# A head's softmax sums inverted and applied in their PSUM bank instead of by way of memory

## The reference

```python
q, k, v = split(xn @ qkvw + qkvb)             # 32 heads of 32 columns
scores = einsum('bhqd,bhkd->bhqk', q, k) / sqrt(32)
ctx = einsum('bhqk,bhkd->bhqd', softmax(scores), v)
x + ctx @ ow + ob + ffn(xn)
```

## Time and profile before

| | |
|---|---|
| median of 3 runs | 2800.13 us (2799.02 to 2804.99) |
| the profiled execution | 2805.34 us |
| its span | 2803.3 us |
| mean granted TensorE clock | 0.955 |
| busy, share of the span | PE 94%, DVE 61%, POOL 56%, ACT 44% |

### The profile page before, as it was taken

One profiled execution on the slowest core, in us unless ns is written; L12 is line 12 of the kernel. 1 busy time (PEld: TensorE's weight loads), 2 busy tenths in 40 slices (PEclk: granted clock), 3 DMA queues, 4 the chain that ended last, 5 costly groups with the idle time before them and its releaser, 6 DMA issues. The chain is left out here.

```text
span 2803.3 us, 34972 instructions
## 1 busy us (share of the span) xinstructions
PE 2646.7 (94%) x13032; PEld 1682.0 (60%) x13032; DVE 1701.0 (61%) x2649; ACT 1234.9 (44%) x2299; POOL 1568.3 (56%) x498
## 2 busy tenths in 40 slices
PE   7999999999799999999999999999999999988999
PEld 6888887778455454554555455455545545526887
DVE  8411111111588888888888878888888888823222
ACT  3111111110066565666566666656666666662100
POOL 0111111011078787888788788878878887871221
PEclk9999999999699999999999999999999999998999
DMA  4233333113546667667666766776676667424332
GB/s 143 87 130 124 116 112 113 67 55 103 139 96 140 127 135 150 141 129 152 142 130 138 151 143 129 148 146 130 139 151 141 131 145 150 102 58 161 116 105 94
DMA packets 168168, 351.01 MB, mean 125 GB/s; under 512 B 89632, under 2 KB 114720, under 8 KB 137376
## 3 DMA queue, kind: packets, MB, share of 16 engines
q0 software_dynamic: 22320, 162.54, 28.9%
q1 hardware_dynamic: 145712, 186.70, 24.0%
HBM read 122.44 MB, written 63.69 MB: 66 GB/s over the span
## 5 line engine op out<-in xcount | busy, mean ns | idle before, releaser
L899 DVE TENSOR_REDUCE part_max<-ps_b 128x1 f32<-128x512 f32 x2048 | 1259.8, 678 | 288.2 <-PE ps_b L778 287.9
L736 POOL TENSOR_TENSOR psum_p<-psum_p,probs 128x2048 f32<-128x2048 f32 x254 | 1189.0, 4681 | 76.9 <-ACT probs L885 66.7
L885 ACT ACTIVATE probs<-ps_b 128x512 f32<-128x512 f32 x1924 | 990.0, 616 | 518.4 <-PE ps_b L767 514.0
L778 PE MATMUL ps_b<-kp,qp 96*128 96x512 f32 x2048 | 878.9, 437 | 108.4 <-DVE part_max L899 93.7
L767 PE MATMUL ps_b<-qp,kp 97*128 97x512 f32 x2048 | 866.1, 426 | 5.2 <-ACT probs L885 5.1
L767 PEld LDWEIGHTS ps_b<-qp,kp 97*128 97x128 f32 x2048 | 400.5, 196 | 343.1 <-issue 207.8
L778 PEld LDWEIGHTS ps_b<-kp,qp 96*128 96x128 f32 x2048 | 414.8, 203 | 249.2 <-DVE part_max L899 182.4
L794 PE MATMUL ps_b<-probs,vh 128*32 128x512 f32 x3848 | 484.5, 618 | 0.0
L236 POOL TENSOR_TENSOR wlo<-wraw,whi 128x1024 fp32r<-128x1024 f32 x29 | 69.5, 2399 | 612.9 <-ACT whi L339 612.9
L265 PE MATMUL ps_a<-xhi,whi 128*128 128x512 f32 (+1 forms) x928 | 370.6, 399 | 1.1 <-DVE elo L428 0.9
L265 PE MATMUL ps_a<-xlo,whi 128*128 128x512 f32 (+1 forms) x928 | 367.8, 396 | 0.0
(11 more groups left out here) (78 smaller groups left out, 1226.4 us busy)
## 6 DMA issues: line engine op xcount, KB each, us to landing
psum_q<-probs POOLq DMA_DIRECT2D x155, 1024.0 KB, 7.6
kp<-qk_scr SPq DMA_DIRECT2D x96, 256.0 KB, 4.1
qp<-qk_scr SPq DMA_DIRECT2D x96, 256.0 KB, 6.3
qk_scr<-ehi SPq DMA_DIRECT2D x16, 1024.0 KB, 3.9
qk_scr<-elo SPq DMA_DIRECT2D x16, 1024.0 KB, 6.7
wraw<-wcat SPq DMA_DIRECT2D x29, 512.5 KB, 7.5
craw<-cz_scr SPq DMA_DIRECT2D x16, 768.0 KB, 5.0
stage<-x SPq DMA_DIRECT2D x16, 512.0 KB, 3.9
```

The source lines that it names most:

```text
L736: pool.tensor_tensor(acc[:, :], first[:, :], tile(h, t)[:, :], ALU.add).then_inc(pool_done, 1)
L778: pe.matmul(ps[:, ring_bank(u), :], qp[s][0:PACK, tn * P:(tn + 1) * P], kp[s][0:PACK, b * NQ:(b + 1) * NQ], start=True, stop=True).then_in ...
L885: act.activation(tile(h, t)[:, b * NQ:(b + 1) * NQ], ps[:, n % ST_BANKS, :], ACT.Exp, scale=SCALE).then_inc(exp_done, 1)
L899: dve.tensor_reduce(part_max[hn % 2][:, tn, b:b + 1], ps[:, ring_bank(u), :], AX_X, ALU.max) \
```

## The change

The reciprocals are taken by VectorE in the PSUM bank that holds the sums, in four quarters of 128 columns, in place. Each quarter of the context is then the product of `raw_ctx` (SBUF) and that bank (PSUM). Both happen in the head after the one they belong to, at steps 7 to 10: the reciprocal after the second block's maximum, the multiply after the fourth's. ScalarE's copy of the sums, the spreading, storing and broadcasting DMAs and their semaphores go, and one of three `raw_ctx` buffers. The bank stays out of the ring until the fourth multiply (step 10), so the maxima of steps 7 to 10 have three banks; which bank comes next is now worked out from a list of unused banks. In the last head four reciprocals of 128 columns take the place of one of 512.

```diff
-SUMS_AT, RECIPROCAL_AT, NORMALISE_AT = 6, 9, 1
+SUMS_AT = 6
+DIVIDE_AT = SUMS_AT + 1
+GIVEN_BACK_AT = DIVIDE_AT + QB - 1
...
-        raw_ctx = [sb(f"raw_ctx{s}", [P, NQ]) for s in range(3)]
+        raw_ctx = [sb(f"raw_ctx{s}", [P, NQ]) for s in range(2)]
...
+                if t == GIVEN_BACK_AT and h >= 1:
+                    ring_order.append(("given back", h - 1, 0, 0))
...
+        ring_bank, ring_before, maxima_until = {}, {}, {}
+        unused = [(RING_BANK + n, None) for n in range(RING_BANKS)]
+        maxima = 0
         for u in ring_order:
-            maxima_until.append(maxima_until[-1] + (u[0] == "max"))
-
-        def ring_bank(u):
-            return RING_BANK + ring_place[u] % RING_BANKS
+            if u[0] == "given back":
+                u = ("sum", *u[1:])
+                unused.append((ring_bank[u], u))
+                continue
+            ring_bank[u], ring_before[u] = unused.pop(0)
+            maxima += u[0] == "max"
+            maxima_until[u] = maxima
+            if u[0] != "sum":
+                unused.append((ring_bank[u], u))
...
             elif kind == "sum":
-                eng.wait_ge(sums_taken, h + 1)
+                eng.wait_ge(ctx_ready, QB * (h + 1))
...
-            def invert_sums(h):
-                sp.wait_ge(sums_taken, h + 1)
-                for b in range(QB):
-                    sp.dma_start(sums_q[b * HD:(b + 1) * HD, :], sums_b[b * HD:b * HD + 1, :]) \
-                        .then_inc(sums_spread, 16)
-                sp.wait_ge(recip_done, h + 1)
-                sp.dma_start(recip_scr.rearrange("(p c) -> p c", p=P), recip_q[:, :]).then_inc(recip_stored, 16)
-                sp.wait_ge(recip_stored, 16 * (h + 1))
-                for b in range(QB):
-                    sp.dma_start(recip_b[b * HD:(b + 1) * HD, :],
-                                 recip_scr[b * NQ:(b + 1) * NQ].partition_broadcast(HD)).then_inc(recip_loaded, 16)
...
-                    if h >= 2:
-                        store_ctx(h - 2)
-                    invert_sums(h - 1)
+                    store_ctx(h - 1)
...
-                    if t == SUMS_AT and h >= 1:
-                        take_sums(h - 1)
...
-            def reciprocal(h):
-                dve.wait_ge(sums_spread, 16 * QB * (h + 1))
-                wait(dve, recip_stored, 16 * h)
-                dve.reciprocal(recip_q[:, :], sums_q[:, :]).then_inc(recip_done, 1)
+            def reciprocal(h, part):
+                c = slice(part * P, (part + 1) * P)
+                bank = ps[:, ring_bank[("sum", h, 0, 0)], c]
+                if part == 0:
+                    dve.wait_ge(sum_ready, h + 1)
+                dve.reciprocal(bank, bank).then_inc(recip_done, 1)
...
-                dve.tensor_tensor(out_ctx[h % 2][:, c], raw_ctx[h % 3][:, c], recip_b[:, c], ALU.mult) \
-                    .then_inc(ctx_ready, 1)
+                dve.tensor_tensor(out_ctx[h % 2][:, c], raw_ctx[h % 2][:, c], ps[:, ring_bank[("sum", h, 0, 0)], c],
+                                  ALU.mult).then_inc(ctx_ready, 1)
...
-                        if b == 1 and h >= 2 and 0 <= t - NORMALISE_AT < QB:
-                            normalise(h - 2, t - NORMALISE_AT)
-                    if t == RECIPROCAL_AT and h >= 1:
-                        reciprocal(h - 1)
+                        if h >= 1 and 0 <= t - DIVIDE_AT < QB:
+                            if b == 1:
+                                reciprocal(h - 1, t - DIVIDE_AT)
+                            if b == 3:
+                                normalise(h - 1, t - DIVIDE_AT)
...
-            dve.reciprocal(recip_b[:, :], ps[:, ring_bank(("sum", LAST, 0, 0)), :]).then_inc(recip_done, 1)
+                reciprocal(LAST, part)
```

More of the change, by code:

```diff
@@ L514, in _, with attend @@
                     dve.tensor_tensor(elo[:, u, c], ps[:, nb, :], gates[:, u, c], ALU.mult).then_inc(lo_done, 1)
-def attend(nc, qk_scr, v_scr, recip_scr, cz_scr, w2, w_early, early_loaded):
+def attend(nc, qk_scr, v_scr, cz_scr, w2, w_early, early_loaded):
     with ExitStack() as ctx:
@@ L564, in attend @@
         sum_ready = sem("sum_ready")
-        sums_taken = sem("sums_taken")
-        sums_spread = sem("sums_spread")
         recip_done = sem("recip_done")
-        recip_stored = sem("recip_stored")
-        recip_loaded = sem("recip_loaded")
         ctx_ready = sem("ctx_ready")
@@ L594, in attend @@
         ring_order.append(("sum", LAST, 0, 0))
-        ring_place = {u: n for n, u in enumerate(ring_order)}
-        maxima_until = [0]
+        ring_bank, ring_before, maxima_until = {}, {}, {}
+        unused = [(RING_BANK + n, None) for n in range(RING_BANKS)]
+        maxima = 0
         for u in ring_order:
-            maxima_until.append(maxima_until[-1] + (u[0] == "max"))
-        def ring_bank(u):
-            return RING_BANK + ring_place[u] % RING_BANKS
+            if u[0] == "given back":
[7 more added lines that the diff above has]
+                unused.append((ring_bank[u], u))
         def maxima_count(u):
-            return maxima_until[ring_place[u] + 1]
+            return maxima_until[u]
         def wait_ring(eng, u):
-            n = ring_place[u] - RING_BANKS
-            if n < 0:
+            before = ring_before[u]
+            if before is None:
                 return
-            kind, h = ring_order[n][:2]
+            kind, h = before[:2]
             if kind == "max":
-                eng.wait_ge(mx_free, maxima_until[n + 1])
+                eng.wait_ge(mx_free, maxima_until[before])
             elif kind == "sum":
-                eng.wait_ge(sums_taken, h + 1)
+                eng.wait_ge(ctx_ready, QB * (h + 1))
             else:
@@ L777, in scores @@
                     pe.wait_ge(kq_loaded[s], 16 * 6 * (hn // SLOTS + 1))
-                pe.matmul(ps[:, ring_bank(u), :], qp[s][0:PACK, tn * P:(tn + 1) * P],
+                pe.matmul(ps[:, ring_bank[u], :], qp[s][0:PACK, tn * P:(tn + 1) * P],
                           kp[s][0:PACK, b * NQ:(b + 1) * NQ], start=True, stop=True).then_inc(mx_ready, 1)
@@ L784, in transpose_max @@
                 wait_ring(pe, u)
-                pe.transpose(ps[0:TT, ring_bank(u), 0:P], row_max[h % 2][:, :], ident[:, :]).then_inc(mx_ready, 1)
+                pe.transpose(ps[0:TT, ring_bank[u], 0:P], row_max[h % 2][:, :], ident[:, :]).then_inc(mx_ready, 1)
             def values(h, t):
@@ L808, in sums @@
                 pe.wait_ge(chained, chain_count(h, CHAIN_TILES[-1]))
-                sum_of(ring_bank(u), psum_q[h % 2], True, False)
+                sum_of(ring_bank[u], psum_q[h % 2], True, False)
                 pe.wait_ge(pool_done, pool_count(h, POOL_TILES[-1]))
-                sum_of(ring_bank(u), psum_p[h % 2], False, True).then_inc(sum_ready, 1)
+                sum_of(ring_bank[u], psum_p[h % 2], False, True).then_inc(sum_ready, 1)
             def last_sums(t):
@@ L816, in last_sums @@
                     wait_ring(pe, u)
-                sum_of(ring_bank(u), tile(LAST, t), t == LAST_ONES_TILES[0], False).then_inc(pv_done, 1)
+                sum_of(ring_bank[u], tile(LAST, t), t == LAST_ONES_TILES[0], False).then_inc(pv_done, 1)
             def step(h, t):
@@ L850, in _ @@
             pe.wait_ge(pool_done, pool_count(LAST, LAST_POOL_TILES[-1]))
-            sum_of(ring_bank(("sum", LAST, 0, 0)), psum_p[LAST % 2], False, True).then_inc(sum_ready, 1)
+            sum_of(ring_bank[("sum", LAST, 0, 0)], psum_p[LAST % 2], False, True).then_inc(sum_ready, 1)
         @block.scalar
@@ L856, in take_raw @@
                 act.wait_ge(pv_done, TT * (h + 1))
[L857 to L863, removed]
+                wait(act, ctx_ready, QB * (h - 1))
+                act.activation(raw_ctx[h % 2][:, :], ps[:, PV_BANK, :], ACT.Copy).then_inc(raw_done, 1)
             def wait_tile(h, t):
@@ L898, in take_max @@
                 dve.wait_ge(mx_ready, maxima_count(u) + flips_before(u))
-                dve.tensor_reduce(part_max[hn % 2][:, tn, b:b + 1], ps[:, ring_bank(u), :], AX_X, ALU.max) \
+                dve.tensor_reduce(part_max[hn % 2][:, tn, b:b + 1], ps[:, ring_bank[u], :], AX_X, ALU.max) \
                     .then_inc(mx_free, 1)
@@ L910, in take_transposed @@
                 dve.wait_ge(mx_ready, maxima_count(u) + h + 1)
-                dve.tensor_scalar(neg_max[h % 2][:, :].bitcast(F32R), ps[0:TT, ring_bank(u), 0:P], -1.0, None,
+                dve.tensor_scalar(neg_max[h % 2][:, :].bitcast(F32R), ps[0:TT, ring_bank[u], 0:P], -1.0, None,
                                   ALU.mult).then_inc(neg_ready, 1)
-            def reciprocal(h):
-                dve.wait_ge(sums_spread, 16 * QB * (h + 1))
-                wait(dve, recip_stored, 16 * h)
-                dve.reciprocal(recip_q[:, :], sums_q[:, :]).then_inc(recip_done, 1)
+            def reciprocal(h, part):
[4 more added lines that the diff above has]
+                dve.reciprocal(bank, bank).then_inc(recip_done, 1)
             def normalise(h, part):
```

(8 more changed lines are left out.)

8 lines of the change are left out of this document (removed).

## The result

The changed kernel takes 2730.05 us (median of 4 runs, 2726.84 to 2731.44) against 2802.56 for the kernel before in the same comparison; the ratio is 0.9739 (95% interval 0.972 to 0.9757). Its profiled execution took 2726.84 us, with a span of 2724.9. The forecast was 2716, with 2688 to 2755 around it.

What follows compares the result with a forecast made beforehand. Busy times name TensorE, held up by VectorE's multiplies stalled beside GpSimd; afterwards GpSimd's DMA chain binds. Terms sum to -84 from the profiled 2805.34 us, so 2721, or 2716 as median; range 2688 to 2755.

Steps and rivals of the forecast that it cites:

- The multiplies: Steps 1 to 4: four two-SBUF-input multiplies, held up by GpSimd, cost 6.5 us a head (54.91 against 48.38).
- The row of the first stage: First-stage instruction with one SBUF and one PSUM input takes its usual 0.75 us beside GpSimd, so new multiply taken as 0.20.
- What was removed counts nothing: ScalarE's copy of the sums, nine small DMAs a head and a 16-column reciprocal: PE waits for none, so no gain.
- The reciprocal: VectorE, steps 7 to 10: 128 columns take about 0.95 us and hold VectorE for 0.87, by the slope.
- The extra 65 ns for a PSUM source: Skill's dearer PSUM source on VectorE: 0.13 us more a pair, some 0.3 a head, sum unmoved.
- The pair: Steps 7 and 8, then 9 and 10: p8, the eighth ring matmul, 1.35 us late each; PE's pace 51.1 us a head.
- rival 3: Clock falls in the new stalls of steps 7 to 10: 55.5 us a head, 2824 us; chance 0.05 in full.
- What is late next: Chain of addition DMAs on GpSimd: landing 11.5 us, period 51.95, PE waits at the sums from head 3.
- The sum: Whole kernel: +2.7 head 1, -83.8 heads 2 to 29, -3.0 head 30, +0.1 head 31; together -84, 2721 us.
- Rival 1: The DMA chain doesn't bind before the sums, PE's 51.1 us a head holds: 2692 us; chance 0.14.
- Rival 2: Work on PSUM dearer: 0.4 us more a reciprocal gives about 53 a head, 2745; chance 0.14 with one slow stretch.
- Rival 4: Multiplies at steps 7 to 10 still held up by GpSimd: 56.5 us a head, 2853 us; chance 0.03.

Runs made afterwards that it cites:

- experiment 7: Changed kernel with GpSimd's order altered (mostly two additions between addition DMAs), query and value loads held until the previous head's tile-14 DMA lands; 2700.05 us.
- experiment 9: The kernel of experiment 7 without the four reciprocals of each head, the multiply being by the sums themselves; one run, 2651.15 us.
- experiment 1: Changed kernel, but the loads of head h + 2 wait until the last addition DMA (tile 14) of head h - 1 has landed; 2715.41 us.
- experiment 6: Changed kernel with another GpSimd order, loads unmoved, reciprocals and multiplies between pairs of steps, bank kept until step 14, negated maxima loaded before context stores; 2727.82 us.
- experiment 8: The edits of experiment 7 and experiment 6 together on the changed kernel; 2680.13 us.
- experiment 4: The kernel of experiment 1 without the four reciprocals of each head, the multiply being by the sums themselves; one run, 2707.44 us.

## Why the prediction was right, point by point

**The multiplies (6.5 us a head).** Right, and shown: they fell from 1612 ns in the mean to 277, and the stalls at steps 1 to 4 and the clock's falls went with them. Experiment 2 puts both inputs back into SBUF, with nothing else but a wait for VectorE's own earlier multiplies, and the stalls return; experiment 3 keeps the way through memory and takes only the two-input multiply away, and most of the gain is there. The row of the first stage on which I rested was the right one. One reading was loose: PE's stop of 0.64 us at 1217.09 lies before the multiply of 4.56 us, which starts at 1218.75. An earlier one, 1.33 us long, goes before it:

```profile
1215.10 1.33 DVE L928 TENSOR_TENSOR out_ctx<-raw_ctx,recip_b 128x128 f32<-128x128 f32 x1
```

The Trainium skill (SBUF — State Buffer, the section on who interferes with whom) says that a VectorE instruction with at most one SBUF input, outside the two-port modes, doesn't contend with GpSimd, and that one with two contends with a GpSimd instruction that reads SBUF; 289 ns as the longest of 128, against 5205 in experiment 2, agrees.

**What was removed counts nothing.** Not contradicted: experiment 3 keeps all of it, and PE has no wait for it there. But the 20.2 us for the negated maxima in that run leave it open whether the small DMAs cost something.

**The reciprocal (0.95 us, holds VectorE for 0.87).** Right: 956 ns and 0.86 to the next start (1209.85 to 1210.71). In PSUM, in place, it costs what the slope of the earlier trace rows gives. The extra 65 ns for a PSUM source, which the prediction worked out from the Trainium skill (VectorE: DVE Perf Modes, the section on the TRN2 errata), isn't seen: the multiply with one input in PSUM takes 277 ns, and with both in SBUF it took 273 at its shortest in the kernel before (229 once in experiment 2).

**The pair, 1.35 us late, 2.70 a head.** Right: 7.19 us a pair, and 51.18 us a head wherever nothing else waits, in heads 1 to 6 of the change and in all 29 of experiment 7. The clock stayed at 1.00 (rival 3 didn't come), and PE's stop at p6 shows as 0.67 us. That about half of the 2.70 is the lost bank is not shown: without the reciprocals 1.22 us are left for the bank and the multiplies together (experiment 9).

**What is late next.** The mechanism is right and its size was a little off. The waits before L788 end with the landing of the addition DMA, as forecast, and experiments 1 and 7 remove them. But the step "the period is 51.95" was mis-sized. I took 11.5 us from tile-14 to tile-3 DMA from the first heads of before (12.1, 11.5 and 11.6); with the same order and loads, in heads 7 to 29 of the change, it was 11.3 to 13.1 and about 12 in the mean, and the heads took 52.40. Against that, heads 2 to 6 had shorter landings (10.6 to 12.0), so that the spare lasted until head 7 and not head 3. In sum heads 2 to 29 took 2340.69 - 879.62 = 1461.1 us for my 1453.7 (879.62 is 828.46 and the first head's 51.16): 7.4 too little.

**The sum.** 2721 against the profiled execution, which gave 2726.84: 7.4 from those heads, less 1.6 from outside them. The rest of the distance to the median isn't in the kernel: I took the profiled execution to lie 5.2 us above the median, as before; after, it lay 3.2 below. That is 8.4 of the 14 us between 2716 and 2730.

**The rivals.** Rival 1 (the chain doesn't bind, 51.1 and 2692) fell; made true by experiment 7 it gives 51.18 and 2700. Rival 2 fell with 956 ns. Its price was wrong besides: by its own rule 0.4 us more on each reciprocal adds 0.4 in the first pair and 0.8 - 0.24 in the second, so 52.1 us a head and not 53, and from 51.1 to 54.91 it takes 2.2 us a reciprocal, not 1.7. Rival 3 fell for stops of 0.67 us. Rival 4, made true by experiment 2, costs even more than I had: 58.9 us a head instead of 56.5. My price was the old mean of the multiplies; at the new place their mean is 1914 ns, and the wait for the negated maxima comes on top.

## What to carry to other kernels

An instruction's mean duration can be a wait: 128 columns don't need 1.6 us here, and a shortest of 0.27 beside a longest of 5 says that something is held. If an engine shares its way to SBUF with a busy neighbour, moving one input to PSUM can be worth more than any saving in work. Before forecasting the gain of a removed stall, take the free head (here head 1) and ask of each other engine what its cycle is at that pace, chained transfers with their landing included; here GpSimd had 6 us idle in each head and was still the bound. And try an improvement behind the next bound only after that bound is moved: the same placement was worth nothing in experiment 6 and 20 us in experiment 8.

## What the runs showed of the hardware

- The start-to-start time of chained 1 MB addition DMAs depends on what else is on the queues: 7.6 us where nothing was loaded beside (1142.70 to 1150.33 in experiment 4), 11.3 to 13.1 beside a head's 1.8 MB of loads (heads 7 to 29 of the change), 14.2 where the loads began just before (1150.33 to 1164.57), with up to 15.1 in other heads of that run.
- A transfer of 8 KB that left 0.94 us behind such a DMA was slow too: 6.1 us to PE's next matmul in experiment 1, where its median landing in the change is 2.3 us.
- TensorE's clock stayed at 2.4 GHz (1.00) through two stops of 0.67 us in every head, and through single ones of up to 2.09 us before the sums (change, head 25):

```profile
2097.31 1.06 PE L788 MATMUL ps_b<-psum_q,ones 128*32 128x512 f32 x8 [2.09 <-DMA psum_q<-probs]
...
2096.00:2098.00 2.00, 0.69 (x8) 0.34 (x12) 0.00 (x0) 0.00 (x0) 0.27 (x1) 1.00 0.02 4
```

- In experiment 2 stops of 1.18, 1.23 and 0.67 us within 9 us went before a fall to 0.50 (1.2 GHz). The fall comes at the end of the stretch from 1335 to 1336, before the fourth stop, of 1.28 us, is over:

```profile
1327.22 0.50 PE L766 MATMUL ps_b<-kp,qp 96*128 96x512 f32 x1 [1.18 <-DVE part_max L880]
1332.65 0.50 PE L766 MATMUL ps_b<-kp,qp 96*128 96x512 f32 x1 [1.23 <-DVE part_max L880]
1334.65 0.50 PE L766 MATMUL ps_b<-kp,qp 96*128 96x512 f32 x1 [0.67 <-DVE part_max L880]
1337.26 0.80 PE L766 MATMUL ps_b<-kp,qp 96*128 96x512 f32 x1 [1.28 <-DVE part_max L880]
...
1335.00:1336.00 1.00, 0.98 (x4) 0.30 (x2) 1.00 (x2) 0.58 (x1) 1.00 (x1) 0.93 0.00 0
1336.00:1337.00 1.00, 0.00 (x0) 0.00 (x0) 1.00 (x2) 0.61 (x2) 1.00 (x2) 0.50 0.00 0
```
